# Edge loop of the first graph layer: work items of 4 destinations, two chains in one PSUM bank

## The reference

```python
xl = (x @ W_l + b_l).reshape(n, HEADS, C)
xr = (x @ W_r + b_r).reshape(n, HEADS, C)
e = (edge_attr @ W_e).reshape(-1, HEADS, C)
g = jax.nn.leaky_relu(xl[src] + xr[dst] + e, NEG_SLOPE)
logits = jnp.einsum('ehc,hc->eh', g, att)
amax = jax.ops.segment_max(logits, dst, num_segments=n)
ex = jnp.exp(logits - amax[dst])
msg = xl[src] * alpha[..., None]            # alpha: ex over its sum per destination
out = jax.ops.segment_sum(msg, dst, num_segments=n)
```

## Time and profile before

| | us |
|---|---|
| median of 3 runs (6216.44 to 6216.94) | 6216.84 |
| the profiled execution | 6213.84 |
| its span | 6212.0 |
| first to last gather of the edge loop (starts) | 363.0 to 2587.3 |
| busy over the span: PE, PEld, DVE, ACT, POOL | 4970.0, 4268.8, 3033.8, 1847.2, 3670.2 |
| mean granted TensorE clock | 0.735 |

### The profile page before, as it was taken

One profiled execution on the slowest core, in us unless ns is written; L12 is line 12 of the kernel. 1 busy time (PEld: TensorE's weight loads), 2 busy tenths in 40 slices (PEclk: granted clock), 3 DMA queues, 4 the chain that ended last, 5 costly groups with the idle time before them and its releaser, 6 DMA issues. The chain is left out here.

```text
span 6212.0 us, 116784 instructions
## 1 busy us (share of the span) xinstructions
PE 4970.0 (80%) x35178; PEld 4268.8 (69%) x35178; DVE 3033.8 (49%) x5092; ACT 1847.2 (30%) x3935; POOL 3670.2 (59%) x3427
## 2 busy tenths in 40 slices
PE   2458999999998998706999867888878887774899
PEld 2336666666666666506999767777877877774899
DVE  9688888888888889655221211111111111112221
ACT  0035555555555555400000022222222222221100
POOL 7667777777777777530000067777777777776000
PEclk9579888888888889757999855555555555555899
DMA  9345555555555555416999566666666666663698
GB/s 350 122 132 162 153 158 160 162 166 165 164 164 155 154 160 168 125 28 237 365 365 366 193 187 212 206 204 197 214 203 209 198 208 205 210 201 95 273 395 326
DMA packets 622991, 1260.53 MB, mean 203 GB/s; under 512 B 131705, under 2 KB 431290, under 8 KB 597220
## 3 DMA queue, kind: packets, MB, share of 16 engines
q10 hardware_dynamic: 206000, 595.93, 30.3%
q1 hardware_dynamic: 307508, 546.42, 24.4%
q0 software_dynamic: 109184, 115.05, 8.8%
HBM read 923.85 MB, written 490.51 MB: 228 GB/s over the span
## 5 line engine op out<-in xcount | busy, mean ns | idle before, releaser
L737 POOL DMA_INDIRECT att_gl<-tab_l,top_zero x1568 | 1743.5, 1112 | 492.9 <-issue 473.4
L1224 POOL DMA_INDIRECT sum_gl<-tab_l,top_zero x1568 | 1547.6, 987 | 520.5 <-issue 477.6
L977 ACT ACTIVATE att_acc<-att_pc 128x392 bf16<-128x392 f32 x2352 | 1077.8, 497 | 1049.6 <-PE att_pc L755 921.6
L1152 PE MATMUL sum_pm<-sum_msg,sum_S 128*128 128x64 f32 x3136 | 681.7, 412 | 389.6 <-ACT sum_msg L1192 389.6
L752 PE MATMUL att_pc<-att_ohl,att_ohv 128*128 128x392 bf16 x2352 | 851.1, 362 | 143.2 <-DVE att_ohl L855 142.7
L1122 DVE TENSOR_TENSOR sum_t<-sum_pb,sum_gl 128x512 f32<-128x512 f32 x196 | 135.5, 691 | 1665.3 <-DMA sum_gl<-tab_l,top_zero 1268.8
L1152 PEld LDWEIGHTS sum_pm<-sum_msg,sum_S 128*128 128x128 f32 x3136 | 656.1, 321 | 422.5 <-ACT sum_msg L1192 218.4
L755 PE MATMUL att_pc<-att_acc,att_ohv 128*128 128x392 bf16 x2352 | 845.5, 359 | 115.4 <-ACT att_acc L977 111.9
L1134 PE MATMUL sum_pb<-sum_wbs,sum_ea 64*128 64x64 f32 x3136 | 694.7, 419 | 29.0 <-DMA sum_ea<-in_ea64T 29.0
L1134 PEld LDWEIGHTS sum_pb<-sum_wbs,sum_ea 64*128 64x128 f32 x3136 | 676.2, 329 | 40.8 <-DMA sum_ea<-in_ea64T 29.4
L771 PEld LDWEIGHTS att_pl<-att_xe,att_S 128*128 128x128 f32 x3136 | 588.1, 213 | 152.5 <-issue 127.8
(11 more groups left out here) (384 smaller groups left out, 5277.2 us busy)
## 6 DMA issues: line engine op xcount, KB each, us to landing
A<-att_acc SPq DMA_DIRECT2D x2352, 98.0 KB
l_a<-A SPq DMA_DIRECT2D x147, 1568.0 KB, 9.2
att_dall<-in_dst ACTq DMA_DIRECT2D x224, 448.0 KB
sum_dall<-in_dst ACTq DMA_DIRECT2D x196, 512.0 KB, 4.9
hop_at<-AT SPq DMA_DIRECT2D x56, 1568.0 KB
sum_a<-A ACTq DMA_DIRECT2D x49, 1568.0 KB
AT<-sum_at ACTq DMA_DIRECT2D x49, 1568.0 KB, 6.4
l_at<-AT SPq DMA_DIRECT2D x42, 1568.0 KB
```

The costliest lines, as they stand in the source:

```text
L737: nc.gpsimd.indirect_dma_start(out=gl[s][:, k * GQ + j, :], out_offset=None, in_=g.tab_l, in_offset=bass.IndirectOffsetOnAxis(ap=g.ix[:, c ...
L977: nc.scalar.activation(acc[c][n % CR][:, :], pc[c][m % 2][:, 0:LO], ACT.Copy).then_inc(s_acc[c], 1)
L1152: mm = nc.tensor.matmul(pm[s][:, j, :], S[h * R + s][:, j, :], msg[h * R + s][:, j, :], start=True, stop=True)
L1224: nc.gpsimd.indirect_dma_start(out=gl[n % RB][:, j, :], out_offset=None, in_=g.tab_l, in_offset=bass.IndirectOffsetOnAxis(ap=g.ix[:, c:c + ...
```

## The change

An item's window is 4 destinations instead of 8. A chunk then needs more items, 3,136 instead of 2,352 over both chains (1,568 each); an item's product has 196 columns instead of 392, since the source range is cut into 32 parts instead of 16. `ohv` stays 128 by 128 by 2 for an item; its compare constant is now taken from the first 128 entries of the constant of `ohl`.

Item m of chain 0 and item m of chain 1 become one pair. Their two products lie in one PSUM bank (columns 0 to 195 and 196 to 391), and one ScalarE copy takes both. Two banks serve the pairs, where four had served the two chains; of the two banks set free, one gives the message sums a second bank. A slot holds 7 pairs, always. VectorE's portions are the first three pairs and the other four, both chains in one instruction. The places of the message sums in the slots are new: one group's sums in each slot. SyncE loads the store rows of a slot's 14 items in one step and issues 3,136 stores of 128 rows of 392 bytes where there were 2,352 of 784 bytes. Ahead of the loop the tables are larger (25 instead of 19 gathers of each kind, 3,200 values per partition), and some of their tiles share memory with others.

```diff
-WIN = 8
+WIN = 4
 HI = P // WIN
 LO = NP // HI
 NW = NP // WIN
 ITEMS = NCH + NW - 1
 IT = (ITEMS + P - 1) // P
+IB = (IT + 3) // 4
 CH = 2
-CI = 1176
-CJ = 6
-CB = 7
-SLOTS = (6, 6, 6, 4, 6, 6, 4, 4)
-CR = 7
+CI = 1568
+CJ = 7
+CR = CJ
...
-        ohv = [[st.sb(f"ohv{c}_{h}", [P, CJ, P, 2], BF16) for h in range(2)] for c in range(CH)]
-        ohl = [[st.sb(f"ohl{c}_{h}", [P, CJ // 2, LO, 2], BF16) for h in range(2)] for c in range(CH)]
+        ohv = [st.sb(f"ohv{h}", [P, CJ, CH, P, 2], BF16) for h in range(2)]
+        ohl = [st.sb(f"ohl{h}", [P, CJ, LO, CH], BF16) for h in range(2)]
...
-        pm = st.ps("pm", [P, 512])
-        pc = [[st.ps(f"pc{c}_{b}", [P, 512]) for b in range(2)] for c in range(CH)]
+        pm = [st.ps(f"pm{k}", [P, 512]) for k in range(2)]
+        pc = [st.ps(f"pc{b}", [P, 512]) for b in range(2)]
...
+                def pair(i, t, m):
+                    n = i * TI + (t * CJ + m)
+                    h, to = t % 2, pc[(t * CJ + m) % 2]
+                    for q, (a, z) in enumerate(PIECES):
+                        if m == a:
+                            pe.wait_ge(s_oh, i * (4 * SL) + (4 * t + 2 * q + 2))
                     if not known(n, 2):
-                        pe.wait_ge(s_acc[c], n + (-1))
...
+                        pe.wait_ge(s_acc, n + (-1))
+                    for c in range(CH):
+                        nc.tensor.matmul(to[:, c * LO:(c + 1) * LO], ohv[h][:, m, c, :, 0], ohl[h][:, m, :, c],
+                                         start=c == 0, stop=False, skip_group_check=True)
+                    wait_reuse(pe, s_acc, n)
+                    for c in range(CH):
+                        mm = nc.tensor.matmul(to[:, c * LO:(c + 1) * LO], ohv[h][:, m, c, :, 1],
+                                              acc[(m - 1) % CR][:, c, :], start=False, stop=c == CH - 1,
+                                              skip_group_check=True)
+                    mm.then_inc(s_mm, 1)
...
-                        for a, z in ((0, 1), (1, SLOTS[t] // 2)):
-                            for c in range(CH):
-                                items(i, t, c, a, z)
+                        for a, z in PIECES:
+                            items(i, t, a, z)
...
+                def count(i, t, m):
+                    wait_reuse(act, s_st[m], i * (16 * CH * SL) + 16 * CH * t)
+                    act.wait_ge(s_mm, i * TI + (t * CJ + m + 1))
+                    nc.scalar.activation(acc[m][:, :, :].rearrange("p c l -> p (c l)"),
+                                         pc[(t * CJ + m) % 2][:, 0:CH * LO], ACT.Copy).then_inc(s_acc, 1)
```

More of the change, by code:

```diff
@@ L624, in edge_loop @@
     R, GH = 2, GB * HEADS
-    at0 = [sum(SLOTS[:t]) for t in range(len(SLOTS) + 1)]
-    PLACE = {6: range(6), 4: (0, 1, 3, 4)}
     SL = R * NQ
+    TI = SL * CJ
+    PIECES = ((0, 3), (3, CJ))
     AHEAD = 2
@@ L802, in turn @@
                         first, second = not known(b, 1), not known(b, 2)
-                        place = PLACE[SLOTS[t]]
                         for m in range(CJ):
-                            if m in place:
-                                for c in range(CH):
-                                    item(i, t, c, place.index(m))
+                            pair(i, t, m)
                             if m == 0:
@@ L991, in turn @@
                             load_dst(i * SL + (t + 3), (k + 3) % NQ)
-                        place = PLACE[SLOTS[t]]
                         for m in range(CJ):
-                            if m in place:
-                                for c in range(CH):
-                                    count(i, t, c, place.index(m))
+                            count(i, t, m)
                             if m == 1 and not (final and t + 3 >= SL):
                                 load_group(i * SL + (t + 3), (k + 3) % NQ, s, i)
-                            if k == 1 and first and m == 4:
+                            if k == 1 and first and m == 5:
                                 weights(b - 1)
-                            if k == 1 and first and m == 5:
+                            if k == 1 and first and m == 6:
                                 by_edge(b - 1, 1 - s, i + (s - 1))
@@ L1004, in turn @@
                                 load_ends(b)
-                            if k == 3 and first and m in (2, 5):
-                                keep_sums(b - 1, 1 - s, m // 3)
-                            if k < 2 and second and m == 3:
-                                keep_sums(b - 2, s, 2 + k)
+                            if k == 3 and first and m in (0, 5):
+                                keep_sums(b - 1, 1 - s, m // 5)
+                            if k == 0 and second and m == 4:
+                                keep_sums(b - 2, s, 2)
+                            if k == 1 and second and m == 2:
+                                keep_sums(b - 2, s, 3)
                 turns(act, TURNS, turn)
@@ L1760, in __init__ @@
         n = IT * P
-        self.hi, self.rkr = (space[:, q * n:(q + 1) * n].rearrange("p (t e) -> p t e", e=P) for q in range(2))
-        self.lor = st.sb("lor", [P, IT, P])
+        self.hi = space[:, 0:n].rearrange("p (t e) -> p t e", e=P)
+        self.lor = rows.sr[:, :, :].bitcast(F32)
         self.pt = [st.ps(f"ipt{k}", [P, 4, P]) for k in range(2)]
@@ L1803, in values @@
         step(v.tensor_scalar(near[:, :], near[:, :], g.dcol1[:, :], -1.0, ALU.mult, ALU.add))
-        step(v.tensor_copy(g.vals[:, :, 1], near[:, 0:NI]))
+        step(v.tensor_copy(g.vals[:, :, :, 1].rearrange("p m c -> p c m"),
+                           near[:, 0:NI].rearrange("p (c m) -> p c m", c=CH)))
         dve.sem_inc(self.s_e, 1)
```

149 lines of the change are left out of this document (70 added, 79 removed).

## The result

The changed kernel takes 6268.0 us in the median (6261.7 to 6269.8, 4 runs), the kernel before 6216.6 beside it: a ratio of 1.0083 (95% interval 1.0066 to 1.0101), 51 us slower. The prediction was 6312, with 6250 to 6390 as the likeliest case's own range. The profiled execution took 6269.75 us, 55.9 more than that of before; its mean granted clock is 0.723 against 0.735.

What follows compares the result with a forecast made beforehand. GpSimd's gathers, lengthened by VectorE's two-input instructions, were taken to bound the loop. Terms of +56, +25, nothing for stores and +14 summed to +95: 6309 us profiled, 6312 median, range 6180 to 6500.

Steps and rivals of the forecast that it cites:

- the likeliest case: Edge loop: gathers get longer behind fewer but longer VectorE instructions; forecast 6312 us, own range 6250 to 6390, chance 0.52.
- The gathers beside VectorE, +56: Edge loop: GpSimd's gathers are held to the end of the running VectorE operand instruction; longer instructions add 56 us.
- the formula: Gathers starting anywhere wait by half the squares of VectorE's instruction lengths, factor 0.89: 9.91 us per group before, 10.16 after.
- factor 1: Upper bound of the gathers' term, no favour from gathers going in step with VectorE: 10.36 us per group, +101 us.
- the rival of 6209 us: Edge loop: holding goes by VectorE's total time, not its instructions' length; -22 + 14 us, so no change; chance 0.09.
- The faster rival: Edge loop: gathers settle into the free part of VectorE's list and get shorter; about 6157 us, chance 0.17.
- TensorE and ScalarE, +25: Edge loop: their chain is just covered by GpSimd; groups where GpSimd's two-group lead runs out add 25 us (0 to +575).
- The round: TensorE and ScalarE's chain for one pair, copy to product to next copy: 0.9 to 0.95 us, 6.7 for 7 pairs.
- the prediction's own sum: TensorE's mean group 1/(f/12.5 + (1 - f)/8.4), f its lower-clock share, expected near 0.45; reaches 10.16 us at 0.53.
- The rival with TensorE at the lower clock as the bound: Edge loop: with a lower-clock share of 0.7 TensorE sets the group at 10.9 us; 6448 us, chance 0.22.
- Stores, nothing: Edge loop: SyncE issues 784 more stores, but a slot's buffer is reused only after 7 pairs, 10 us; no added time.
- Ahead of the loop, +14: Before the loop: six more destination gathers add 2 us, VectorE's longer table arithmetic and copies 12; together 14 us.

Runs made afterwards that it cites:

- three portions: The changed kernel with VectorE's operands built in portions of 3, 2 and 2 pairs in place of 3 and 4: 6201 us, ratio 0.9966 to the kernel before.
- one portion: The kernel before with one operand portion per chain and slot in place of two: 6304 us, ratio 1.0133 to the kernel before.
- single pairs: The kernel before with every operand portion one pair, 2 or 3 portions per chain and slot in place of 2: 6240 us, ratio 1.0031.
- seven portions: The changed kernel with its operands built pair by pair, seven portions of one pair in place of 3 and 4: 6164 us, ratio 0.9912 to the kernel before.
- five portions: The changed kernel with portions of 1, 1, 1, 2 and 2 pairs in place of 3 and 4: 6154 us, ratio 0.9899 to the kernel before.
- the last run: The changed kernel with operands built in the loop's first pass only, later passes using what stands in the buffers: 6111 us, ratio 0.9837 to the kernel before.
- four and five portions: The changed kernel with portions of 1, 2, 2 and 2 pairs: 6174 us; with portions of 1, 1, 1, 2 and 2: 6154 us.

## Why the prediction was right, and where its working was off

*The gathers beside VectorE, +56.* Right in mechanism and size: 10.16 us per group in the formula and in the trace, +51.6 us from first to last gather since the kernel before stood at 9.93, where the formula has 9.90. The size was helped by balance: the traces have +49 us behind operands, +12 behind S and logits and -5 behind `messages`; the formula has about +59 and -2, and leaves `messages` out. Its upper bound was worked out too high: with factor 1 the formula gives about 10.3 and +90 us, not 10.36 and +101; the measured 10.16 lies below both. The three things that the term rests on were tested apart: the lengths (three portions, one portion), not the total time (three portions and one portion go against it, and with it goes the rival of 6209 us), not the stores. Its one weak premise, "a gather may start anywhere", fails where VectorE's list repeats in short equal rounds, so that gathers fall into step with it (rounds of 0.81 us with single pairs before, 0.61 with seven portions). The faster rival rested on just that, gathers that settle into a free part of the list; it was not so with portions of 3 and 4, but it is with seven, and in part with five (82 us behind operands, 126 by the formula).

*TensorE and ScalarE, +25.* This step failed: it measured nothing. The lead does not run out: GpSimd waits 2.4 us for messages in all, where the same view of before had 6.6, and "issue" is 475.3 of its idle time, as it was 473.4. The round was sized right: 0.94 us between two copies (1211.77 and 1212.71 in ScalarE's timeline), and none between 500 and 2400 us follows the last sooner than 0.93.

```profile
1211.77 0.50 ACT L978 ACTIVATE att_acc<-att_pc 128x392 bf16<-128x392 f32 x1 [0.61 <-PE att_pc L757]
1212.71 0.50 ACT L978 ACTIVATE att_acc<-att_pc 128x392 bf16<-128x392 f32 x1 [0.44 <-PE att_pc L757]
```

Two things were off. The 25 us did not come out of the sum: at the expected share of 0.45 it gives 9.85 us, already below 10.16, and they were put on top for groups in which the lead runs out. And the share was too high. I expected 0.45; from 500 to 2400 us the granted clock is 0.83, and with levels of 0.5 and 1 that is a share of 0.34 (0.28 before, at 0.86). By the prediction's own sum that is 1/(0.34/12.5 + 0.66/8.4) = 9.5 us, below 10.16: covered. The windows from 500 to 2400 us, of before, of the changed kernel and of the last run:

```profile
500.00:2400.00 1900.00, 1710.97 (x9822) 1204.89 (x9821) 1637.51 (x3087) 1056.33 (x2369) 1488.90 (x1336) 0.86 0.56 161
500.00:2400.00 1900.00, 1567.93 (x10951) 1255.20 (x10950) 1524.99 (x2292) 791.35 (x1681) 1501.53 (x1307) 0.83 0.63 158
500.00:2400.00 1900.00, 1581.08 (x11789) 1260.74 (x11790) 917.81 (x1657) 849.68 (x1805) 1437.25 (x1420) 0.89 0.69 170
```

The clock did fall with TensorE's busy time, from 0.86 with 1,711 us to 0.83 with 1,568, but the last run has 0.89 with 1,581, a share of 0.22. The sum gives 9.05 us there and the loop took 9.39, most of it GpSimd's, so no run measures the sum itself. The rival with TensorE at the lower clock as the bound falls with it.

*Stores, nothing.* So it came out, though a new wait stands in ScalarE's list, between 500 and 2400 us:

```profile
ACT att_acc L978 <- DMA A<-att_acc: 55.5, 28, 5.3
```

In the kernel before it was 3.6 us. "A slot's buffer is used again after 7 pairs, 10 us: nothing" counted the transfers and not SyncE's queue; the gathers' lead covers it at this pace. It is 115 and 125 us with four and five portions, so it is a bound that comes near.

*Ahead of the loop, +14.* 10.7 measured. The arithmetic was sized right: the steps on 3,200 values take 1.83 and 3.49 us where 1.43 and 2.69 scaled give 1.88 and 3.54.

```profile
226.79 1.83 DVE L1783 TENSOR_SCALAR tab_hT<-tab_hT 128x3200 f32<-128x3200 f32 x1
228.66 3.49 DVE L1784 SCALAR_TENSOR_TENSOR items_sr<-tab_hT,items_sr 128x3200 f32<-128x3200 f32 x1
```

*After the loop.* No term; it gave back 6 us, which no run takes apart.

So the forecast's first term called the sign and nearly all of the size. The 44 us between 6312 and 6268 are the 25 that did not come, 4 of the first term, 3 ahead of the loop, 6 behind it and 5 of the profiled executions' distances to their medians.

## What to carry to other kernels

Where GpSimd's gathers set the pace, look at the lengths of VectorE's two-input instructions and not at their total time: five portions instead of two make this kernel 1.8% faster (6154 for 6268 us), though VectorE does more. Shorter is not always better: single pairs made the kernel before slower (6240 for 6217) and gained nothing over five portions in the changed one. Work taken off engines that are not the bound brought nothing here, and what came with it, longer instructions on one of them, cost 52 us. When a wait depends on where two periodic lists meet, look at a timeline of a few rounds before believing an average, and after cutting a list finer, look for a standstill at the loop's head.

## What the runs showed of the hardware that I had not expected

- It is the start that decides whether a gather waits. Over all the traces, each of the 2,519 gathers that started 0.04 to 0.3 us into an operand instruction with at least 0.25 us left was held to its end, and 2 of the 242 that started in the instruction's first 0.02 us. An `ohv` instruction of one pair that starts together with a gather takes 0.03 us longer (0.445 for 0.412 us in the median, seven portions), and the ones behind it run beside the same gather at their usual length.
- At the head of a pass VectorE's next instruction came 2.7 to 3.7 us behind the branch in the kernels with 150 and 178 VectorE instructions in a pass, and 0.24 us (median) behind it in those with 146 and fewer. That its list is read again there is argued from the instruction transfers.
- One store costs SyncE 0.479 us on the mean when it waits for nothing, its share of reading the store rows included, and 28 of them a group made it the slowest engine of the loop.
